# An FFN with block-scaled rounding on one core: GpSimd adds and stores the residual of the last group but one, the idle products at the start are fewer, and W's second half is rounded tile by tile

## The reference

```
y = einsum('bct,bcd->bdt', x, table[itok])
a = quant_dequant_mxfp4(y);  w = quant_dequant_mxfp4(W)   # blocks of 32 along the last axis
out = x + (einsum('mk,nk->mn', a, w) + bias)
```

## Time and profile before

| what | value |
|---|---|
| median of 3 runs | 96.53 us (96.41 to 96.92) |
| the profiled execution's own time | 96.33 us |
| its span, first to last instruction | 94.3 us |
| PE, DVE, ACT, POOL busy | 82.1, 83.3, 74.7, 30.4 us |
| granted TensorE clock, mean | 0.986 |

### The profile page before, as it was taken

One profiled execution on the slowest core, in us unless ns is written; L12 is line 12 of the kernel. 1 busy time (PEld: TensorE's weight loads), 2 busy tenths in 40 slices (PEclk: granted clock), 3 DMA queues, 4 the chain that ended last, 5 costly groups with the idle time before them and its releaser, 6 DMA issues.

```text
span 94.3 us, 2149 instructions
## 1 busy us (share of the span) xinstructions
PE 82.1 (87%) x704; PEld 41.5 (44%) x711; DVE 83.3 (88%) x148; ACT 74.7 (79%) x86; POOL 30.4 (32%) x57
## 2 busy tenths in 40 slices
PE   4999996996699998999899979989989999999600
PEld 4995573692382334332433433343334344345300
DVE  1189977999999999999999999999999999999900
ACT  3745099997977959999999999999999997956000
POOL 4478895997887103000200410040003003030000
PEclk9999999999999999999999999999999999999995
DMA  0899799999999999999899996589179859939894
GB/s 16 301 324 281 102 374 326 355 348 282 338 311 282 331 311 252 216 276 242 199 248 296 332 255 116 222 200 217 40 255 241 167 214 240 210 81 281 317 296 148
DMA packets 14683, 23.20 MB, mean 246 GB/s; under 512 B 4178, under 2 KB 4946, under 8 KB 14674
## 3 DMA queue, kind: packets, MB, share of 16 engines
q1 hardware_dynamic: 11744, 17.83, 63.2%
q0 software_dynamic: 2256, 4.21, 21.2%
q10 hardware_dynamic: 674, 1.05, 3.9%
HBM read 11.54 MB, written 8.39 MB: 211 GB/s over the span
## 4 chain that ended last, share of the span: by engine, by line
PE 45%; ACT 11%; DVE 8%; issue 7%; DVEq 0%; ACTq 0%
PE o_ps L378 22%; PE y_ps L331 6%; ACT o_sb L528 5%; PE o_ps L373 4%; ACT y_sb L507 4%; PE y_ps L378 4%; PE o_ps L359 2%; PE o_ps L343 2%; DVE last_x L807 2%; DVE top L694 2%; DVE a L703 1%; DVE x_sb L802 1%; PE o_ps L405 1%; PE y_ps L359 1%; PE y_ps L343 1%
## 5 line engine op out<-in xcount | busy, mean ns | idle before, releaser
L378 PE MATMUL o_ps<-wT,aT 128*128 128x512 bf16 x98 | 23.5, 380 | 1.0 <-issue 1.0
L675 DVE TENSOR_TENSOR n_int<-y_sb,inv 128x1024 int16<-128x1024 f32 (+1 forms) x18 | 19.7, 1102 | 0.3
L307 POOL DMA_DIRECT2D x_sb<-o_sb x6 | 6.1, 1017 | 41.9 <-ACT o_sb L528 41.9
L331 PE MATMUL y_ps<-x_sb,mix 64*64 64x512 f32 x128 | 16.8, 609 | 3.2 <-ACT y_sb L507 3.2
L499 ACT ACTIVATE z<-y_ps 128x1024 bf16<-128x1024 bf16 x16 | 16.2, 1036 | 4.2 <-PE y_ps L331 3.9
L203 POOL DMA_DIRECT2D mix<-in_L_cond_weights_dram x32 | 16.7, 522 | 5.7 <-issue 4.2
L405 PE MATMUL o_ps<-idle 128*128 128x128 bf16 x218 | 16.8, 240 | 1.2 <-DVE idle L708 1.2
L507 ACT COPY y_sb<-y_ps 128x1024 f32<-128x1024 f32 x16 | 16.2, 1030 | 0.0
L405 PEld LDWEIGHTS o_ps<-idle 128*128 128x128 bf16 x218 | 14.6, 108 | 3.6 <-issue 3.2
L378 PEld LDWEIGHTS o_ps<-wT,aT 128*128 128x128 bf16 x104 | 9.1, 98 | 12.0 <-issue 2.7
L694 DVE TENSOR_TENSOR top<-zone,s 128x2048 bf16<-128x2048 bf16 (+2 forms) x14 | 11.7, 839 | 1.3 <-ACT zone L515 1.2
(11 more groups left out here) (59 smaller groups left out, 76.6 us busy)
## 6 DMA issues: line engine op xcount, KB each, us to landing
x_sb<-in_x_dram SPq DMA_DIRECT2D x7, 1024.0 KB, 10.2
out_dram<-x_sb SPq DMA_DIRECT2D x16, 256.0 KB, 3.4
x_sb<-o_sb POOLq DMA_DIRECT2D x6, 512.0 KB, 5.5
out_dram<-x_sb SPq DMA_DIRECT2D x5, 512.0 KB, 2.8
w_sb<-in_L_ffn_weight_dram SPq DMA_DIRECT2D x4, 256.0 KB, 3.6
last_x<-in_x_dram SPq DMA_DIRECT2D x4, 256.0 KB, 8.2
x_sb<-in_x_dram SPq DMA_DIRECT2D x1, 512.0 KB, 5.8
mix<-in_L_cond_weights_dram SPq DMA_DIRECT2D x32, 16.0 KB, 7.1
```

Source lines behind the costliest of these rows:

```text
L331: last = nc.tensor.matmul(y_ps[HALVES[g], 2 * q + r, :], mix[HALVES[r], (step - 1) * GROUP + n, :], x_tiles(step, n)[HALVES[r], :], start= ...
L378: last = nc.tensor.matmul(o_bank(step, t), aT[:, t, c, :], wT[:, c, :], start=False, stop=(c == KC - 1))
L675: nc.vector.tensor_tensor(columns(n_int, t, n), columns(y_sb[:, step % 2, :, :], t, n), columns(inv, t, n), ALU.mult).then_inc(n_done, 1)
```

## The change

Three edits are made together. The first is the residual of group 7: PE no longer adds x there, ACT copies all four tiles as they are into a new buffer `late_sb` (`copy_late(0)` and `copy_late(1)`), POOL adds x to each pair in SBUF and starts its store, and DVE and SP have no work for group 7's output any more. Pair 0 of the group is turned over in the other layout for that. The second: WARMUPS is 20. The third: W's second half is rounded by two instructions of one tile each, with `tree_1(1)` between them, and `tree_2(4)` and `tree_3(4)` move ahead. `n_done` counts one more from then on, and the waits on it are raised by one.

```diff
-WARMUPS = 24
+WARMUPS = 20
...
-            for step in range(1, LAST):
-                if step < LAST - 1:
-                    sp.wait_ge(pair_copied, 2 * step)
-                else:
-                    sp.wait_ge(late_copied, 2)
+            for step in range(1, LAST - 1):
+                sp.wait_ge(pair_copied, 2 * step)
...
-            for t in range(SUMMED, GROUP):
-                sp.wait_ge(added, t - SUMMED + 1)
-                store(LAST - 1, t)
...
+            for q in range(2):
+                pool.wait_ge(late_copied, 2 * q + 2)
+                pair = x_tiles(LAST - 1, 2 * q, 2)
+                nc.gpsimd.tensor_tensor(pair, late_sb[:, 2 * q:2 * q + 2, :].rearrange("p t n -> p (t n)"), pair, ALU.add
+                                        ).then_inc(late_added, 1)
+                pool.wait_ge(late_added, q + 1)
+                n0 = (LAST - 2) * GROUP + 2 * q
+                pool.dma_start(out_dram[:, n0:n0 + 2, :], pair.rearrange("p (n t) -> p n t", n=2)
+                               ).then_inc(late_stored, 16)
...
-            turn_pair(LAST - 1, 0, straight=True)
-            residual_pair(LAST - 1, 0)
+            turn_pair(LAST - 1, 0)
             for t in range(2):
-                bias_tile(LAST - 1, t, start=False)
+                bias_tile(LAST - 1, t)
...
-            copy_late()
+            copy_late(0)
             copy_turned_last(0)
             zone_pair(after(LAST), late_part(1), GROUP - 1, 1)
-            for t in range(1, GROUP):
+            copy_turned_last(1)
+            copy_late(1)
+            for t in range(2, GROUP):
                 copy_turned_last(t)
...
-            round_w(1)
+
+            round_w(2, 1)
+            tree_1(1)
+            round_w(3, 1)
+            tree_2(4)
             limit(0, 2, 2, 2)
-            tree_1(1)
-            rescale(0, 2, 2, 2, 2)
-            tree_2(4)
             tree_3(4)
+            rescale(0, 2, 3, 2, 2)
             block_max(3)
...
-            for t in range(SUMMED, GROUP):
-                dve.wait_ge(o_ready, tiles_done(LAST - 1, t))
-                nc.vector.tensor_tensor(x_tiles(LAST - 1, t), o_bank(LAST - 1, t), x_tiles(LAST - 1, t), ALU.add
-                                        ).then_inc(added, 1)
```

More of the change, by code:

```diff
@@ L66, in adaln_ffn_program @@
         x_sb = sb("x_sb", [P, TILES * T], F32)
+        late_sb = sb("late_sb", [P, GROUP, N], F32)
         last_x = sb("last_x", [P, GROUP, T], F32)
@@ L101, in adaln_ffn_program @@
         x_in = [sem(f"x_in_{s}") for s in range(STEPS + 1)]
[L102 removed]
+        last_x_in, late_added = sem("last_x_in"), sem("late_added")
         sp_mix_in = [sem(f"sp_mix_in_{s}") for s in range(STEPS + 1)]
@@ L254, in _ @@
                     store(step, SUMMED, GROUP - SUMMED)
-            for t in range(SUMMED, GROUP):
-                sp.wait_ge(added, t - SUMMED + 1)
-                store(LAST - 1, t)
             for t in range(GROUP - 1):
-                sp.wait_ge(added, t + 3)
+                sp.wait_ge(added, t + 1)
                 store_last(sp, t, 0, slice(0, N), stored)
             for half in range(2):
-                sp.wait_ge(added, GROUP + 2 + half)
+                sp.wait_ge(added, GROUP + half)
                 store_last(sp, GROUP - 1, 0, n_half(half), stored)
-            sp.wait_ge(stored, 16 * (2 * (LAST - 1) + LAST - 3 + 2 + GROUP + 1))
+            sp.wait_ge(stored, 16 * (2 * (LAST - 2) + LAST - 3 + GROUP + 1))
             sp.wait_ge(others_stored, 16 * (GROUP + 1))
-            sp.wait_ge(late_stored, 16)
+            sp.wait_ge(late_stored, 16 * 3)
         @block.gpsimd
@@ L503, in y_pair @@
                 if step > 2:
-                    act.wait_ge(n_done, 2 * (step - 2) + q + 1)
+                    act.wait_ge(n_done, 2 * (step - 2) + q + 2)
                 act.wait_ge(y_ready, tiles_done(step, 2 * q + 1))
@@ L528, in copy_out, with copy_late @@
                 nc.scalar.copy(o_sb[:, step % 2, :, :], o_ps[:, SUMMED:GROUP, :]).then_inc(copied_out, 2)
[L530 to L533, removed]
+            def copy_late(q):
+                act.wait_ge(o_ready, tiles_done(LAST - 1, 2 * q + 1))
+                nc.scalar.copy(late_sb[:, 2 * q:2 * q + 2, :], y_ps[:, 2 * q:2 * q + 2, :]).then_inc(late_copied, 2)
             def copy_turned(step, q):
@@ L598, in _ @@
                 zone_pair(after(LAST), late_part(1), t, 1)
-            copy_late()
+            copy_late(0)
             copy_turned_last(0)
             zone_pair(after(LAST), late_part(1), GROUP - 1, 1)
-            for t in range(1, GROUP):
+            copy_turned_last(1)
+            copy_late(1)
+            for t in range(2, GROUP):
                 copy_turned_last(t)
             for t in range(GROUP - 1):
-                act.wait_ge(added, t + 3)
+                act.wait_ge(added, t + 1)
                 store_last(act, t, 1, slice(0, N), others_stored)
             for half in range(2):
-                act.wait_ge(added, GROUP + 2 + half)
+                act.wait_ge(added, GROUP + half)
                 store_last(act, GROUP - 1, 1, n_half(half), others_stored)
@@ L682, in other_zones, with round_w @@
                                         -1, EXPONENT - 2 * BINADE, ALU.mult, ALU.add).then_inc(other_zone_done, 1)
[L684 to L687, removed]
+            def round_w(t, n):
+                dve.wait_ge(inv_done, t // 2 + 1)
+                nc.vector.tensor_tensor(blocked(columns(n_int, t, n)), by_place(w_sb[:, t * K:(t + n) * K]),
+                                        blocked(columns(inv, t, n)), ALU.mult).then_inc(n_done, 1)
             def limit(step, zones, t=0, n=GROUP):
@@ L723, in _ @@
             tree_1(0, 2, 2, z_count=GROUP)
-            round_w(0)
+            round_w(0, 2)
             tree_2(3, 2, 2)
@@ L758, in _ @@
                     tree_2(step + 4)
-                    rescale(step, after(step), 2 * step + 2)
+                    rescale(step, after(step), 2 * step + 3)
                     tree_3(step + 4)
@@ L781, in _ @@
             tree_3(LAST + 3)
-            rescale(LAST - 1, late_part(0), 2 * LAST, 0, 2)
+            rescale(LAST - 1, late_part(0), 2 * LAST + 1, 0, 2)
             block_max(LAST + 2)
@@ L785, in _ @@
             lowest_zone(LAST + 2)
-            rescale(LAST - 1, late_part(1), 2 * LAST, 2, 2)
+            rescale(LAST - 1, late_part(1), 2 * LAST + 1, 2, 2)
             lift(LAST, LAST + 2)
@@ L795, in _ @@
                 round_y(LAST, t, 1)
-                rescale(LAST, late_part(1 + t), 2 * LAST + t, t - 1, 1)
+                rescale(LAST, late_part(1 + t), 2 * LAST + 1 + t, t - 1, 1)
                 limit(LAST, after(LAST) + t, t, 1)
-            rescale(LAST, late_part(1 + GROUP), 2 * LAST + GROUP, GROUP - 1, 1)
-            for t in range(SUMMED, GROUP):
-                dve.wait_ge(o_ready, tiles_done(LAST - 1, t))
-                nc.vector.tensor_tensor(x_tiles(LAST - 1, t), o_bank(LAST - 1, t), x_tiles(LAST - 1, t), ALU.add
-                                        ).then_inc(added, 1)
+            rescale(LAST, late_part(1 + GROUP), 2 * LAST + 1 + GROUP, GROUP - 1, 1)
             dve.wait_ge(last_x_in, 16 * GROUP)
```

## The result

The changed kernel takes 99.72 us (median of 8, 99.21 to 102.36), the kernel before beside it 96.81: the ratio is 1.0285, with an interval of 1.0244 to 1.0327. The change is 2.9% slower. The forecast was slower too, but by 1.0 us where 2.8 to 2.9 were measured, and the time lies outside its range.

The account below looks back on a forecast made before the run. The prediction took a chain mostly of PE and ACT to bound the body, and the last store's landing the end. POOL's chain, 2.1 us later less 0.9 from the start, added 1.2 to 96.33: 97.5 us, range 95.0 to 98.6.

Parts of the forecast that it names:

- The start: Before the body: fewer idle products and W rounded tile by tile let the body begin 0.9 us earlier (0.4 to 1.0).
- The 0.9 us: Lead of the body from both edits at the start, kept to its exit and taken off the new end.
- the step that took 0.4 us from the idle products: First mixing: four loops fewer bring it forward until a table's landing stops it; 0.4 us, bounds 0 and 0.5.
- Where POOL gets in beside DVE: End of the kernel: POOL's first addition enters at 84.8, old clock, in the gap after DVE's rescale.
- One addition: POOL's addition of 128x1024 in f32 at the end: 2.4 us, taken between 1.5 and 2.6.
- POOL is held by the accumulating DMA of group 6 until 83.45: Start of POOL's chain at the end: after this DMA, POOL issues group 6's store until 84.21, old clock.
- DVE's branch: Last group: limit and rescale wait behind POOL's addition until 87.2, then work some 1.7 us later; stores land near 93.4, not last.
- POOL's branch: End: two additions and two stores on POOL in line, last landing at 95.1 against 93.9, 1.2 us later.
- a sign of being wrong: Stated test at the end: the prediction is wrong if POOL's stores of 512 KB land in 3 to 4 us.
- Faster: Rival at the end: POOL's additions are short and the last group's stores end the kernel, 94.8 us; chance 0.30.
- DVE keeps POOL out: Rival at the end: POOL gets in only behind the last rescale, its chain 1.1 us later, 98.6 us; chance 0.10.
- The edits at the start do nothing: Rival at the start: ACT or a load holds the body anyway, POOL's chain costs 2.1, 98.4 us; chance 0.05.

Follow-up runs that it names:

- e9: The changed kernel itself, run once more for a profile of an undisturbed execution: 99.31 us.
- e2: The kernel before with only the idle products cut from 24 to 20 loops: 96.53 us, ratio 0.997.
- e8: The kernel before with both edits at the start (20 loops, W's second half rounded in two) and no change at the end: 95.71 us, ratio 0.989.
- e3: The kernel before with only W's second half rounded tile by tile, 24 loops: 95.52 us, ratio 0.991.
- e4: The changed kernel with WARMUPS back at 24 loops: 99.94 us, ratio 1.036 against the kernel before.
- e7: The changed kernel with 24 loops and POOL's first addition only, the second pair stored without the sum: 97.99 us, ratio 1.015 against the kernel before.
- e5: The changed kernel with 24 loops, without POOL's additions; POOL stores ACT's copies as they are: 96.19 us, ratio 0.995 against the kernel before.
- e10: The changed kernel with 24 loops, without POOL's additions, ACT's copies stored by SP as soon as they are there: 94.58 us, ratio 0.977 against the kernel before.
- e6: The changed kernel with 24 loops, POOL's additions made to wait for DVE's last rescale: 99.37 us, ratio 1.029 against the kernel before.
- the added wait: One more wait on SP, forcing its stores beside the next accumulating DMA: 97.4 us in the kernel before, 99.85 in the changed one with 24 loops.

## Why the prediction was wrong

**The start.** Right, a little low. Mixing at 10.05 was forecast, 10.04 seen in e9; block maximum 16.35 and 16.27; turn of group 1 25.2 and 25.07. The body kept this lead, as was forecast: group 6's accumulating DMA was issued at 77.08 in e9 and at 78.14 before. The 0.9 us hold for e9. They don't hold on average: the step that took 0.4 us from the idle products rested on one execution's landing of a table, and e2 and e8 measured nothing for them. From the timed runs the start is worth 1.1% together (e8), 0.9% of it W's (e3). Where POOL gets in beside DVE was right too: 84.8 was forecast, less what the start gains, which in e4 was 0.2 (25.97 for the turn of group 1). The addition is recorded from 84.06 there, but with 2.36 taken off its end it starts at 84.46, near the end of the rescale (84.62).

**One addition.** 2.4 us was taken between 1.5 and 2.6; it is 2.36. The two-input rows were the right ones, though they are of 32 elements and gave a range, from which 2.4 was a choice.

**The step that failed** is "POOL is held by the accumulating DMA of group 6 until 83.45", with DVE's branch "not last". It failed in two ways, in two kinds of execution:

- With the late landing (e9), POOL starts 2.0 us later than the 83.9 forecast, since the DMA takes 7.7 instead of 5.0 us (2.7 more, less the 0.6 for which POOL was to wait for DVE's gap, and 0.2 more lead). The rest of the sum comes out: 97.5 + 2.0 = 99.5, measured 99.31. Part of that is luck. From the first addition to the second store's issue took 6.1 us where 5.8 were forecast, as the semaphore behind each addition took 0.30 and not 0.1, and the landing took 5.1 and not 5.4. The 5.0 came from a trace in which nothing collided; the 10.4 of the earlier trace rows is group 1's DMA, and the sum left it out.
- With the early landing (e4), POOL slips into DVE as I took it to, but DVE is held a second time, by the second addition, which I had running beside free DVE instructions; and PE, idle for 4.37 us behind it, comes back at a granted clock of 0.51. I had 1.7 us for this branch, on the assumption that DVE stands behind POOL's addition, which no row of the kernel before shows; e4 shows it, with a limit of 2.58 us where 0.43 is usual, and e7, with 2.55; DVE's last addition came 5.6 us later than before. The exclusion was costed once and ended once, and the clock was priced only at the start. POOL's branch was not last in e4: its stores landed in 3.2 and 3.4 us, not in 5.4, which the prediction itself had named as a sign of being wrong.

Both branches were in the text: POOL's was 2.0 us too short in e9, DVE's about 4 in e4. That POOL's stores land late was in the chain as 5.4, and in e9 the second store took 5.1; what I missed is that they also seem to delay the last group's stores (e5 against e10, 1.6 us), which matters where these end the kernel.

**Rivals.** Faster fell with the 2.36. "DVE keeps POOL out" (98.6) has e9's tail, but for another reason: POOL came too late to meet DVE. "The edits at the start do nothing" is half right. The range was too narrow above, since no case let two of them come together.

## What to carry to other kernels

Before work is put on an engine that is idle for most of the span, follow what it waits for at that moment and what stands behind it: here the new additions stood behind a DMA landing that varied from 5.0 to 7.7 us, and ran one behind the other with stores between. Count an exclusion once for each instruction that can hold (in e4 both additions held DVE), and ask what the engine behind the held one does to its clock (PE's was 0.51 there, behind 4.37 us of idling). W's second half rounded tile by tile with the next group's tree between is worth keeping by itself: e3 at 95.52 us is 0.9% faster than the kernel before and faster still than the changed one.

## What the runs showed of the hardware that was not expected

- An addition on POOL of 128x1024 in f32 takes 2.35 to 2.37 us when DVE isn't in its way (e9, e6), and a DVE instruction with two SBUF inputs that starts under it ended 0.3 us behind it (e4: 0.43 became 2.58 and 3.32). DVE's additions from PSUM with one SBUF input ran beside it at their usual 0.69 (e9).
- The accumulating DMA of 512 KB landed in 5.0 to 5.6 us in the kernel before, behind group 1's, and in 7.3 to 8.5 in e9 beside stores of 1 MB. In the four profiles that had it late without the added wait, it stayed late from group 2 or 3 to the end (6.6 to 8.6 us). What tips an execution into it isn't settled.
- 4.37 us of idle PE were followed by a granted clock of 0.51 (e4), and 2.49 us at the start by 0.50 (the changed kernel's first profile); 1.01 us (e9), 1.36 (e8) and 1.43 (e2) at the same place were followed by 1.00.
